# The mask bias of an attention kernel written by ACT instead of TensorE, and three steps moved

## The reference

```python
def layer0(x, y, ...):                    # 8 heads of 32 channels, attention over channels
    q = conv1x1(Wq, bq, y); k = conv1x1(Wk, bk, y); v = conv1x1(Wv, bv, x)
    scores = einsum('bhdl,bhel->bhde', q, k) / sqrt(E)
    out = einsum('bhde,bhel->bhdl', softmax(scores), v)
    o = conv1x1(Wo, bo, out) + x
    return group_norm(o) * gn_w + gn_b    # mean and variance over channels and time
def layer1(x, q, k, v, masks, ...):       # q = k = v = ctx, in chunks of 64 time steps
    scores = einsum('bnqhd,bnkhd->bnhqk', qh, kh) / sqrt(32)
    scores = scores + where(mask > 0, 0.0, -1e9)     # one value per key of the chunk
    out = softmax(scores) @ vh
    out = (out @ W_out.T + b_out).T * masks + x
    return (out - mean(out, time)) * rsqrt(var(out, time) + eps)
```

## Time and profile before

| what | value |
|---|---|
| median of 3 runs | 1559.06 us (1558.3 to 1560.88) |
| the profiled execution, its own time | 1557.83 us |
| its span | 1556.0 us |
| busy: PE, PEld, DVE | 1527.3, 1287.2, 1324.1 us |
| busy: ACT, POOL | 999.5, 451.4 us |
| mean granted TensorE clock | 0.996 of full speed |
| mask matmuls L326 | 512, busy 52.2 us |
| score matmuls L337 | 8192 records, busy 140.7 us |

### The profile page before, as it was taken

How to read it: one execution, slowest core, us unless ns; L and a number is a source line. 1 busy time by engine, 2 the same in 40 slices (tenths; PEclk the granted TensorE clock), 3 DMA queues, 4 the chain that set the end, 5 groups by cost and what they waited for, 6 DMA issues and landing times.

```text
span 1556.0 us, 55525 instructions
## 1 busy us (share of the span) xinstructions
PE 1527.3 (98%) x24660; PEld 1287.2 (83%) x24660; DVE 1324.1 (85%) x2028; ACT 999.5 (64%) x1808; POOL 451.4 (29%) x294
## 2 busy tenths in 40 slices
PE   9999999999999999999999999999999999999995
PEld 7888888888888888888888888888888888888874
DVE  5778888888898888988888888888888889898897
ACT  5656665666656667566575665766666665666655
POOL 1114133141331414214142241423314133141331
PEclk9999999999999999999999999999999999999998
DMA  7132331424324242241433415234142331424221
GB/s 256 54 96 77 110 123 41 145 84 117 110 67 133 70 142 86 83 123 63 143 83 103 124 45 151 88 98 123 49 150 79 120 111 55 133 82 127 59 72 67
DMA packets 96399, 157.33 MB, mean 101 GB/s; under 512 B 5408, under 2 KB 38304, under 8 KB 96032
## 3 DMA queue, kind: packets, MB, share of 16 engines
q1 hardware_dynamic: 96160, 153.78, 32.0%
HBM read 120.20 MB, written 33.55 MB: 99 GB/s over the span
## 4 chain that ended last, share of the span: by engine, by line
PE 86%; DVE 12%; issue 1%; ACT 1%; POOL 0%; ACTq 0%; POOLq 0%; DVEq 0%
PE pj_ps L313 41%; PE l_ps L313 12%; PE l_ps L433 7%; PE s_ps L337 7%; PE w_ps L348 7%; PE w_ps L366 6%; DVE o_sb L994 3%; PE s_ps L326 2%; PE l_ps L450 2%; DVE row_sum L851 1%; DVE prob L846 1%; DVE x_lo L829 1%; DVE y_lo L820 1%; DVE u_sb L868 1%; DVE m_lo L907 1%
## 5 line engine op out<-in xcount | busy, mean ns | idle before, releaser
L1125 POOL TENSOR_TENSOR prob<-prob,row_inv 128x1024 f32<-128x1024 f32 x128 | 258.3, 2018 | 903.8 <-DVE row_inv L856 903.8
L668 ACT CAST att_hi<-w_ps 128x256 fp32r<-128x256 f32 x256 | 82.9, 376 | 227.4 <-PE w_ps L366 221.0
L313 PE MATMUL pj_ps<-y_hi,w_hi 128*128 128x512 f32 x510 | 206.8, 405 | 0.0
L313 PE MATMUL pj_ps<-y_hi,w_lo 128*128 128x512 f32 x510 | 201.3, 395 | 0.0
L313 PE MATMUL pj_ps<-y_lo,w_hi 128*128 128x512 f32 x510 | 201.2, 394 | 0.0
L851 DVE TENSOR_REDUCE row_sum<-prob 128x16 f32<-128x1024 f32 x128 | 154.9, 1210 | 52.1 <-ACT prob L650 52.1
L839 DVE TENSOR_REDUCE row_max<-s_ps 128x16 f32<-128x1024 f32 x128 | 155.9, 1218 | 33.7 <-PE s_ps L337 31.1
L645 ACT COPY prob_t<-w_ps 128x512 f32<-128x512 f32 x256 | 149.8, 586 | 14.2 <-PE w_ps L348 11.4
L1142 POOL TENSOR_TENSOR o_sb<-o_sb,u_sb 128x1024 f32<-128x1024 f32 x60 | 157.9, 2642 | 2.6 <-ACT o_sb L658 2.6
L824 DVE TENSOR_TENSOR yt_hl<-yt_raw,yt_hl 128x1024 fp32r<-128x1024 f32 x64 | 119.8, 1872 | 42.7 <-ACT yt_hl L613 40.8
L846 DVE TENSOR_TENSOR prob<-s_ps,row_max 128x1024 f32<-128x1024 f32 x128 | 155.4, 1214 | 0.1
(11 more groups left out here) (141 smaller groups left out, 3540.0 us busy)
## 6 DMA issues: line engine op xcount, KB each, us to landing
y_raw<-in_ctx SPq DMA_DIRECT2D x64, 512.0 KB, 4.8
yt_raw<-in_ctx_t SPq DMA_DIRECT2D x64, 512.0 KB, 4.8
x_raw<-in_x SPq DMA_DIRECT2D x64, 512.0 KB, 5.3
out_z<-o_sb SPq DMA_DIRECT2D x60, 512.0 KB, 3.6
mask_b<-in_mask SPq DMA_DIRECT2D x64, 256.0 KB, 4.0
out_z<-o_sb SPq DMA_DIRECT2D x8, 256.0 KB, 2.6
u_sb<-in_w SPq DMA_DIRECT2D x2, 512.0 KB, 5.8
w_sb<-in_w SPq DMA_DIRECT2D x1, 1024.0 KB, 11.1
```

Of the source, the lines that this page charges most:

```text
L313: last = mm(dst, lhs, rhs, start=i == 0, stop=i == len(todo) - 1)
L1125: nc.gpsimd.tensor_tensor(cut, cut, row_inv[:, u % 2, :].unsqueeze(2).to_broadcast([P, 2 * HEADS, CHUNK]), ALU.mult).then_inc(probs_done, 1)
```

## The change

- TensorE no longer forms the bias. `neg_rows` and its copies are gone. DVE's `flags` now writes 0 or the large negative number itself in fp32 (a comparison and a multiplication in the same instruction), and ACT copies that row, broadcast, into the two banks of `s_ps` (`preset_mask`, 2 copies of 128 x 512 a unit). The 32 score matmuls add to what stands there (`start=False`). They wait for `mask_set`. `preset_mask` of the next unit stands right behind `exponents` of this one, and waits for that unit's `shifted`, as TensorE did before.
- ACT's `copy_lower` goes from the beginning of slot 7 to slot 6 ahead of the exponents, `copy_u0` from behind the exponents of slot 10 to ahead of them.
- On DVE the steps of M (`layer0` at slot 11) go ahead of `result` in that slot. TensorE waits for `o_bias_done` only ahead of the second half of the output, ACT ahead of its first copy.
- At the start one of six matmuls that open the banks is gone, and TensorE's wait behind them. In the last sample x's third and fourth blocks are loaded one slot earlier, and DVE's `top(6)` and `att_low(4)` go ahead of `split_x(1)` and `shift(6)`.

The core of the diff:

```diff
-        neg_rows = sb("neg_rows", [P, CHUNK], BF16)
-        blocked = sb("blocked", [P, 2, BT], BF16)
+        blocked = sb("blocked", [P, 2, BT])
...
@@ SP, body
+                        if last and load == load_x:
+                            q += 1
...
@@ TensorE, scores(n, u)
                 if e == 0:
                     pe.wait_ge(qkv_copied, count(n, 24, 6 * b + 3))
-                    pe.wait_ge(blocked_done, count(n, 4, b))
-                if exists(n, 8, u - 1):
-                    pe.wait_ge(shifted, count(n, 8, u - 1))
-                for i in range(4):
-                    r, h = divmod(i, 2)
-                    rows = slice(DH * i, DH * i + DH)
-                    mm(s_ps[64 * h:64 * h + 64, r].rearrange("p j g c k -> p j g (c k)"), neg_rows[rows, :],
-                       blocked[rows, b % 2, e * UT:(e + 1) * UT].rearrange("p (j t) -> p j t", j=2).unsqueeze(2).to_broadcast([DH, 2, HALVES, P]),
-                       start=True, stop=False)
+                pe.wait_ge(mask_set, count(n, 8, u))
...
-                                      start=False, stop=t == 3 and g == HALVES - 1)
+                                      start=False, stop=True, skip_group_check=True)
...
@@ TensorE, layer0_output(n, q)
                 if q == 0:
                     pe.wait_ge(m_lo_done, count(n, 1, 0))
-                    pe.wait_ge(o_bias_done, count(n, 1, 0))
                 for o in range(HALVES):
+                    if q == 0 and o == 1:
+                        pe.wait_ge(o_bias_done, count(n, 1, 0))
...
@@ TensorE, start
-            for i in range(6):
+            for i in range(5):
                 last = mm(s_ps[:, i % 2].rearrange("p j g c k -> p (j g c k)"), zeros[:, 0:P], zeros, start=True, stop=True)
             last.then_inc(banks_open, 1)
-            pe.wait_ge(banks_open, 1)
...
@@ ACT
+            def preset_mask(n, u):
+                b, e = divmod(u, 2)
+                if e == 0:
+                    act.wait_ge(blocked_done, count(n, 4, b))
+                if exists(n, 8, u - 1):
+                    act.wait_ge(shifted, count(n, 8, u - 1))
+                else:
+                    act.wait_ge(banks_open, 1)
+                for r in range(2):
+                    last = copy(s_ps[:, r].rearrange("p j g c k -> p j g (c k)"),
+                                blocked[:, b % 2, e * UT:(e + 1) * UT].rearrange("p (j t) -> p j t", j=2).unsqueeze(2).to_broadcast([P, 2, HALVES, P]))
+                last.then_inc(mask_set, 1)
...
@@ ACT, body
-                    if s == S_SUM + 1:
-                        copy_lower(n)
...
                     if e == 0 and not (first and u == 0):
                         copy_pt(n, u - 1, 0)
+                    if s == S_SUM:
+                        copy_lower(n)
+                    if s == S_U:
+                        copy_u0(n)
                     if e == 0:
                         exponents(n, u)
+                        preset_mask(n, u + 1)
                     if j == 1 and not (last and b + 2 >= BLOCKS):
                         split_y(n, b + 2)
-                    if s == S_U:
-                        copy_u0(n)
...
@@ DVE, flags
-                nc.vector.tensor_scalar(blocked[:, b % 2, :], mask_b[:, b % 4, :], 0.0, None, ALU.is_le).then_inc(blocked_done, 1)
+                nc.vector.tensor_scalar(blocked[:, b % 2, :], mask_b[:, b % 4, :], 0.0, NEG / SCALE1, ALU.is_le, ALU.mult).then_inc(blocked_done, 1)
...
@@ DVE, body
+                    if s == S_M:
+                        layer0(n, s)
                     if not first and T_FINAL <= s < T_FINAL + BLOCKS:
                         result(n - 1, s - T_FINAL)
                     if s == S_SC + 1:
                         layer0_inverse(n)
-                    layer0(n, s)
+                    if s != S_M:
+                        layer0(n, s)
...
@@ DVE, tail of the last sample
+            top(n, 6)
+            att_low(n, 4)
             split_x(n, 1)
-            top(n, 6)
             shift(n, 6)
-            att_low(n, 4)
```

More of the change, by code:

```diff
@@ L152, in build @@
         wqk_in, wvo_in, cols_in, consts_in, w0_in = sem("wqk_in"), sem("wvo_in"), sem("cols_in"), sem("consts_in"), sem("w0_in")
-        neg_done = sem("neg_done")
-        zeros_set, banks_open = sem("zeros_set"), sem("banks_open")
+        zeros_set, banks_open, mask_set = sem("zeros_set"), sem("banks_open"), sem("mask_set")
         consts_done = sem("consts_done")
@@ L525, in _ @@
             last.then_inc(c1_ready, 1)
-            pe.wait_ge(neg_done, 1)
             pe.wait_ge(w0_in, 2 * 16)
@@ L680, in copy_output @@
                     act.wait_ge(stored[q], count(n - 1, 1, 0, 16))
+                if q == 0:
+                    act.wait_ge(o_bias_done, count(n, 1, 0))
                 for o in halves:
@@ L721, in _ @@
                 copy_k(0, 0, g)
+            preset_mask(0, 0)
             for m in range(2):
@@ L787, in _ @@
             copy_output(n, 1)
+            preset_mask(n, 7)
             split_x(n, 3)
@@ L1004, in _ @@
             flags(0, 0)
-            dve.wait_ge(consts_in, 16)
-            for i in range(4):
-                last = nc.vector.tensor_copy(neg_rows[DH * i:DH * i + DH, :], cst[0:DH, C_NEG:C_NEG + CHUNK])
-            last.then_inc(neg_done, 1)
             split_y(0, 1)
```

2 lines of the change are left out of this document (1 added, 1 removed).

## The result

The changed kernel takes **1541.93 us** (median of 4 runs, 1541.33 to 1542.93), the kernel before 1559.15 us (4 runs, 1558.30 to 1560.88): ratio 0.9886, 95% interval 0.9874 to 0.9898. It is faster by 17.2 us. The forecast was 30.9 us, so the time lies inside the range that was given (1519 to 1545) and 13.7 us above the predicted one. The profiled execution took 1542.93 us, the longest of the four, with a span of 1541.1 us, 14.9 us less than the span before.

A forecast was written before the change was run, and what follows sets the result against it. TensorE was taken as the bound, busy 98% of the span, with 86% of the chain. Terms -26.9 - 6.5 - 1.5 + 4.0 = -30.9 us gave 1528.2 us from the median 1559.06, range 1519 to 1545.

The forecast's parts named there:

- Part 1: Mask matmuls removed from TensorE: 0.21 us won in each of 128 units, 26.9 us (13.7 to 30.7).
- Part 2: M's steps ahead of result on DVE in slot 11: TensorE's wait for o_bias goes, 15 x 0.43 = 6.5 us won.
- Part 3: Start and tail: 0.3 us won at the start, 1.2 us of the tail's att_low wait, together 1.5 us (0 to 2.1).
- the lost lock: POOL starting before DVE's yt_hl and holding the exclusive SBUF lock; forecast for slot 3 only, TensorE stalling 1.1 us in 15 samples.
- Part 4: ACT's 256 new copies of 128 x 512 into PSUM: 0.25 us stall in each of 16 samples, 4.0 us lost.
- X: Time that one unit's two mask copies hold ACT's queue: 1.0 us taken, 0.9 at the low end.
- stall of 0.25 us in slots 8 to 10: Copies use up ACT's reserve, att_hi ends 0.14 us later, TensorE waits 0.25 us a sample, 4.0 us in all.
- TensorE wants it at 833.96: Slots 8 to 10: TensorE's need for DVE's output, 834.17, moved 0.21 us earlier, against a DVE end of 834.21.
- Rival 1: Slot 3: ACT's later yt_hl lets POOL's join take the lock before DVE; 20 us more, 1548 us; chance 0.15.
- Rival 2: Score weight loads fully open, 0.13 us: each unit wins 0.11 us, 13.7 instead of 26.9 us, 1541 us; chance 0.12.
- Rival 3: Slower: ACT becomes the bound at X = 1.63, 2.7 us a sample lost against 2.1 won, 1567 us; chance 0.06.
- Rival 4: TensorE's saved time comes back as waits for DVE: time within 3 us of before; chance 0.05.

The follow-up runs named there:

- e4: Kernel before, with only M's split ahead of a result on DVE and the waits for o_bias moved as in the change: 1557.50 us, ratio 0.9985.
- e1: Changed kernel without ACT's two mask copies per unit, the mask left out of the scores: 1536.53 us, ratio 0.9841 to the kernel before.
- e2: Changed kernel with 13 more TensorE instructions (idle waits) in slot 13, so blocks end at the same place in every sample: 1536.09 us, ratio 0.9840.
- e10: e9 with SP's loads held back as in e5: 1532.93 us, ratio 0.9827 to the kernel before.
- e6: e2 with DVE's split of the attention output (att_low) ahead of the row maximum in slot 8: 1537.06 us, ratio 0.9845 to the kernel before.
- e11: e9 with a third ACT copy ahead of each pair, into a spare tile nobody reads: 1571.16 us, ratio 1.0071 to the kernel before.
- e9: Changed kernel with 13 more TensorE instructions in slot 13 from sample 1 on and POOL's first scaling behind DVE's split of yt: 1533.33 us, ratio 0.9828.
- e3: Changed kernel with ACT's normalisation of the first block moved behind its copy of the transposed probabilities: 1541.10 us, ratio 0.9872 to the kernel before.
- e5: Changed kernel with SP's loads of slots 3, 4 and 8 held until the scores of units 2 and 4: 1537.73 us, ratio 0.9853.

## Why the prediction was right, and where it was not

**Part 1, the mask matmuls.** Right in mechanism, 0.03 us a unit too high in price. The open weight load is 0.06 us (1.03 to 1.09 us), twice the 0.03 that I took; the five units that nothing else holds (0, 1, 2, 5 and 7) are 0.15 to 0.19 us shorter, not 0.21. That is 26.9 forecast and some 21 to 23 us measured (an estimate, 128 units of 0.17 to 0.18 us). The 53 ns of the Trainium skill ("TensorE: Matmul & The Clock Gate", "LDWEIGHTS (loading the stationary operand)"), which stood in the prediction as the other price, agree with the 0.06.

**Part 2, o_bias.** 0.43 us a sample forecast, 0.44 measured in e4 and in the changed kernel (0.59 less unit 6's own 0.15), but in 14 samples and not 15: the earlier trace rows have 14 waits, and the last sample had none. So it is 6.2 us for 6.5. What I did not see is that M's order alone costs some 2 us of waits in the tail, and more with the low clock behind them (e4).

**Part 3, start and tail.** Wrong in sign. The tail was to give 1.2 us. The wait for `att_lo` is gone, but TensorE now waits 1.1 us for ACT's `o_sb` instead, and 0.6 us came (unit 6 of the last sample takes 13.20 for 13.96 us, 0.15 of it the unit's own); ACT's last pair of copies costs 0.7 us there (e1). Behind the last scores 1.0 us was lost. It is not the instruction gap of 0.54 us that lies there, since e2 and e10 have none and take as long (33.65 and 33.67 us, for 33.67 here); they wait 0.56 and 0.58 us for DVE's `att_lo` instead. Without ACT's copies it is 33.21 us (e1) and before it was 32.7, so half of this loss goes with the copies and the other half stays open. At the start nothing of the 0.3 us came: TensorE's first unit began at 18.92 us before and at 18.91 now. Then 1.2 us were lost in sample 0 by the lost lock.

**Part 4, ACT's copies.** X = 1.0 us was right: a pair holds ACT for 1.03 us (0.52 from one start to the next, twice). The stall of 0.25 us in slots 8 to 10 did not come. Units 3 and 4 do gain less than the others, by 0.04 and 0.13 us. The 0.04 go with the copies (e1 has 10.61 for 10.65), but unit 4 gains just as little without any copy; there it is DVE's `att_lo` (e6), which ended 0.05 us ahead of TensorE's need before and is late as soon as TensorE is faster. So 0.17 us a sample are lost where I had 0.25, and 0.13 of them for another reason. The step that failed is "TensorE wants it at 833.96": I moved TensorE's need by one unit's saving, and not that of DVE, whose slots 8 to 11 are full.

**The rivals.** Rival 1 did not come in slot 3. DVE got in ahead of POOL's join with 0.16 us to spare, where 0.2 was worked out (sample 8 of the changed kernel):

```profile
793.57 1.28 DVE L832 TENSOR_TENSOR yt_hl<-yt_raw,yt_hl 128x1024 fp32r<-128x1024 f32 x1 [1.78 <-ACT yt_hl L603]
793.73 5.72 POOL L1149 TENSOR_TENSOR o_sb<-o_sb,u_sb 128x1024 f32<-128x1024 f32 x2
```

e11 shows the rival with its price: 1.13 us of waiting where 1.1 was forecast. Rival 2 was the truer price of the load in part, 0.06 of 0.13 us. Rival 3 gave 2.7 us a sample for X = 1.63; e11 has that X and loses 2.5, but in other places: 1.7 in unit 2 where slot 3 was to cost 1.3, and nothing in unit 4. Rival 4 is out: the time fell by 1.1%, clear of noise. In unit 4 of each sample, though, its mechanism is what happened: TensorE's saved time comes back as a wait for DVE.

**What was not in it.** 8.0 us of instruction gaps and low clock, half of the 16 us that the stretches of the table fall short. e9, which has next to none of them and not the loss in sample 0, is 9 us faster. None of my steps looked at the instruction queue. It can be seen in the trace of before, which had 195 such fetches. In bursts the closest of them began 2.5 us ahead of their block's end, and TensorE needs 2.3 to 2.4: the cover was a tenth of a microsecond. And one, begun at 821.22 us in unit 4 of sample 8, 1.87 us ahead of its block's end in the large matmuls, already cost 0.18 us: TensorE went on at 823.50, 2.28 us behind its start. The total came into the range because that range reached to 1545 for rivals 1 and 2, neither of which came as written. The forecast itself, with its 0.62, reached to 1535 only. The number was partly luck: right for reasons that are only partly its own.

**Open.** Why before's fetches began some 1.6 us behind the sequencer's release, and e1's 2.2 to 2.9 us behind the same release and the same loads, is not settled. Nor is it shown how much of the 8.0 us each cause would cost by itself, since their effects don't add: e1 and e3 took away one, e5 the other.

## What to carry to other kernels

Price a removed instruction by starts, not by its record, and add what it had hidden: here a weight load of 0.06 us stood open where 0.03 had been allowed. Where an engine runs through 256 short instructions faster than a fetch takes (here 1.9 us against 2.3 to 2.4), look at the instruction queue: a change of a few instructions per iteration can move a block's end into such a burst, a dozen idle waits can move it out again, and large loads issued just ahead of the burst make it worse. Before calling an engine's slack used up, take its work away, and then add to it: without ACT's copies 0.07 us changed in the steady sample, with half as much again the kernel was slower than before the change.

## What the runs showed of the hardware that was not expected

- TensorE's instructions come in packets of 16 KB, 256 each, in the same DMA engines as the data. It went on 2.3 to 2.4 us after a packet's start in nine of the changed kernel's eleven gaps (2.6 and 2.9 in the others, 2.1 to 3.0 in the other runs), though the packet itself took 0.9 to 1.1 us in ten of the eleven and 1.4 in the one of 2.9.
- A gap of 1.48 us was followed a microsecond later by a granted clock of 0.51 over 3.3 us, and cost 3.13 us in all; gaps of 1.22 us in the same trace and of 1.45 us in e1 were not, and those of 0.2 to 0.8 us cost no more than their length.
- Two waits that are met beforehand go into one instruction, and 13 such instructions in a stretch of large matmuls showed no cost (e2, e9).
- DVE that comes 0.3 to 0.5 us behind POOL's start takes 2.7 to 3.0 us for what takes 1.23 alone; and when it waits behind one POOL instruction it goes ahead of the next (2.19 us in the earlier trace rows).
